# Expert loops: register loads of the experts' numbers without range checks, and from a shifted copy of the table on two engines

## The reference, cut to what matters

```python
# L0: 8 experts, 2 chosen, hidden 256
probs = softmax(tokens @ router_w.T); rw, re = top_k(probs, 2); rw = rw / rw.sum(-1)
out = tokens
for e in range(8):
    out = out + combine[:, e:e+1] * (gelu(tokens @ w1[e] + b1[e]) @ w2[e] + b2[e])

# L1: 32 experts, 1 chosen, hidden 64
idx = argmax(xf @ router_w.T + router_b)
out = relu(relu(xf @ W1[idx] + b1[idx]) @ W2[idx] + b2[idx])

# L3: 16 experts, 2 chosen, hidden 512
topk_vals, topk_idx = top_k(x @ gate_w + gate_b, 2); topk_w = softmax(topk_vals)
y = x + sum_k topk_w[k] * (relu(x @ w1[e_k] + b1[e_k]) @ w2[e_k] + b2[e_k])
out = layernorm(y) * gamma + beta
```

## Time and profile before

| | |
|---|---|
| time of the kernel before, median of 3 runs | 3055.85 us (3051.97 to 3062.43) |
| the profiled execution: its span, first to last instruction | 3096.4 us |
| expert loop of m0, from the first product's start on | about 1199 to 1368 us of the span |
| expert loop of m1, scatters included | about 1847 to 1953 us |
| expert loop of m3 | about 2785 to 3030 us |
| TensorE busy over the whole span | 2449.8 us (79%) |
| GpSimd / VectorE / ScalarE busy | 1747.5 / 1477.2 / 1096.0 us |

### The profile page before, as it was taken

How to read it: one execution, slowest core, us unless ns; L and a number is a source line. 1 busy time by engine, 2 the same in 40 slices (tenths; PEclk the granted TensorE clock), 3 DMA queues, 4 the chain that set the end, 5 groups by cost and what they waited for, 6 DMA issues and landing times. The chain is left out here.

```text
span 3096.4 us, 41425 instructions
## 1 busy us (share of the span) xinstructions
PE 2449.8 (79%) x12303; PEld 1613.2 (52%) x12304; DVE 1477.2 (48%) x4878; ACT 1096.0 (35%) x2433; POOL 1747.5 (56%) x1310
## 2 busy tenths in 40 slices
PE   3344438999999985757979959599897999959994
PEld 1122213444455454656858845387465454548883
DVE  8899976655432255236553452533335000163335
ACT  7799962232210023334433323332334000022223
POOL 4887878888887854657848723485510300034443
PEclk9999999999999997978989969799998999969997
DMA  9989969998869952244535433453402544166664
GB/s 325 298 277 298 277 195 280 278 267 233 202 117 312 291 156 69 85 144 123 112 87 124 91 96 89 143 120 73 124 1 66 163 125 136 52 222 198 200 200 143
DMA packets 391819, 525.78 MB, mean 170 GB/s; under 512 B 161964, under 2 KB 302554, under 8 KB 381645
## 3 DMA queue, kind: packets, MB, share of 16 engines
q1 hardware_dynamic: 238142, 460.63, 43.9%
q0 software_dynamic: 127728, 41.96, 13.6%
q10 hardware_dynamic: 25760, 20.90, 2.0%
HBM read 346.64 MB, written 176.71 MB: 169 GB/s over the span
## 5 line engine op out<-in xcount | busy, mean ns | idle before, releaser
L658 POOL DMA_INDIRECT table_pairs<-sums,index_to x392 | 626.4, 1598 | 164.4 <-issue 120.0
L658 POOL DMA_INDIRECT table_t<-sums,index_from x392 | 619.4, 1580 | 122.7 <-issue 118.6
L1708 PE MATMUL sum_psum<-wide,parts 128*128 128x512 f32 x1800 | 434.0, 396 | 6.9 <-DVE parts L1744 3.0
L1708 PEld LDWEIGHTS sum_psum<-wide,parts 128*128 128x128 f32 x1800 | 342.1, 190 | 81.7 <-DVE parts L1744 3.9
L1264 PE MATMUL sum_psum<-abuf,y 128*128 128x512 f32 (+1 forms) x700 | 305.9, 572 | 28.8 <-DMA abuf<-table_pairs 26.5
L1264 PE MATMUL sum_psum<-abuf,acc 128*128 128x512 f32 (+1 forms) x700 | 296.4, 563 | 0.4 <-ACT partial L1217 0.3
L977 PE MATMUL sum_psum<-abuf,y 128*128 128x512 f32 (+1 forms) x700 | 272.5, 549 | 17.9 <-ACT y L868 17.9
L534 PE MATMUL merge_psum<-part,acc 128*128 128x6 bf16 x980 | 71.0, 167 | 239.3 <-DVE pass_on L608 147.1
L1570 ACT ACTIVATE wide<-abuf 128x512 fp32r<-128x512 f16 (+1 forms) x264 | 148.6, 573 | 250.9 <-PE sum_psum L1708 226.3
L534 PEld LDWEIGHTS merge_psum<-part,acc 128*128 128x128 bf16 x980 | 56.9, 104 | 322.5 <-issue 320.2
L2424 PE MATMUL m_x_yp<-m_kept_w,m_x_h 128*128 x736 | 188.5, 394 | 37.5 <-ACT m_x_h L2485 24.8
(11 more groups left out here) (507 smaller groups left out, 4346.6 us busy)
## 6 DMA issues: line engine op xcount, KB each, us to landing
abuf<-table_pairs SPq DMA_DIRECT2D x240, 512.0 KB
table_pairs<-zero SPq DMA_DIRECT2D x50, 1600.0 KB
abuf<-table_counts SPq DMA_DIRECT2D x90, 640.0 KB
table_t<-zero SPq DMA_DIRECT2D x25, 1600.0 KB
abuf<-table_t SPq DMA_DIRECT2D x150, 256.0 KB, 2.7
m_x_wa<-in_L_ffn_w_dram SPq DMA_DIRECT2D x64, 512.0 KB
table_counts<-peeled ACTq DMA_DIRECT2D x150, 128.0 KB
tokens<-y SPq DMA_DIRECT2D x15, 640.0 KB
```

The costliest lines, as they stand in the source:

```text
L658: nc.gpsimd.indirect_dma_start(table[:, :], bass.IndirectOffsetOnAxis(ap=index[:, g, j:j + 1], axis=0), k.sums[:, g, j, 0:width], None, co ...
L1708: mm = nc.tensor.matmul(k.sum_psum[:, b % 2, f, 0:n], parts[:, v, c, f * P:(f + 1) * P], k.wide[:, j % WIDENED, 0:n], start=(c == 0 and v ...
```

## The change

It does three things.

1. `experts_from` and `values` pass a reason to skip the run-time range checks. The checks behind every register load of m0, m1 and m3 go, on all engines.
2. A second table `k.slot_late` holds the same numbers one element later, written by a second VectorE operation in `route` (m0 and m3). TensorE and VectorE load from it at c, which gives them the numbers of the tiles c - 1 to c + 2. The first load of each loop still comes from `k.slot_expert`. The wait that stood behind the single write of the table goes as well; a later wait covers both.
3. ScalarE in m0 loads eight numbers instead of six (`DEEP + DEEP * held`).

```diff
@@ route @@
-                    link(nc.vector.tensor_scalar(k.slot_expert[0:1, 0:m.tiles], rt_psum[0:1, 0:m.tiles], float(E - 1), None,
-                                                 ALU.min))
+                    for to in (k.slot_expert[0:1, 0:m.tiles], k.slot_late[0:1, 1:1 + m.tiles]):
+                        nc.vector.tensor_scalar(to, rt_psum[0:1, 0:m.tiles], float(E - 1), None, ALU.min)\
+                            .then_inc(s["split"], 1)
+                    link.n += 2
@@ run_experts @@
-    def experts_from(engine, c, most=DEEP):
+    def experts_from(engine, c, most=DEEP, late=False):
 
         count = min(most, n - c) if isinstance(c, int) else most
+        table = k.slot_expert if not late else k.slot_late
         return nc.values_load_multi_w_load_instructions(
-            k.slot_expert[0:1, bass.ds(c, count)], engines=[engine], min_val=0, max_val=E - 1)[1]
+            table[0:1, bass.ds(c, count)], engines=[engine], min_val=0, max_val=E - 1,
+            skip_runtime_bounds_check_because=CLAMPED)[1]
...
-                        experts[:] = [None] * start + list(experts_from(mybir.EngineType.PE, c if start else c - 1))
+                        experts[:] = [None] * start + list(experts_from(mybir.EngineType.PE, c, late=not start))
...
-                        experts[:] = experts_from(mybir.EngineType.Activation, c, DEEP + SOONER * held)
+                        experts[:] = experts_from(mybir.EngineType.Activation, c, DEEP + DEEP * held)
...
-                        experts[:] = [None] * start + list(experts_from(mybir.EngineType.DVE, c if start else c - 1))
+                        experts[:] = [None] * start + list(experts_from(mybir.EngineType.DVE, c, late=not start))
@@ run_pairs @@
         return nc.values_load_multi_w_load_instructions(table[0:1, c:c + min(DEEP, n - c)], engines=[engine], min_val=0,
-                                                        max_val=top)[1]
+                                                        max_val=top, skip_runtime_bounds_check_because=CLAMPED)[1]
@@ build @@
         k.slot_expert = held(ctx, "slot_expert", [1, SLOT_TILES], I32)
+        k.slot_late = held(ctx, "slot_late", [1, SLOT_TILES + 2], I32)
```

More of the change, by code:

```diff
@@ L73 @@
 LN_EPS = 1e-5
+CLAMPED = "the tables hold whole numbers from 0 to the bound for any input"
 def over(eng, n, ways, body, last_apart=False, peeled=1):
```

## The result

The changed kernel takes 3032.2 us (median of 4 runs, 3030.7 to 3040.4), the kernel before 3053.9 us (3051.9 to 3062.4): ratio 0.9934, interval 0.992 to 0.9949, which is some 20 us less (16 to 24). The prediction was 3029 us, and 26.5 us less.

What follows compares the result with a forecast made beforehand. TensorE was taken to bound m3 and mostly m1, engines waiting for each other m0. Gains of 10.8 (m3) + 8 (m1) + 13 (m0) = 31.8 us, less a sixth, 26.5, gave 3029 us from 3055.85; range 3010 to 3046.

Steps and rivals of the forecast that it cites:

- the sixth taken off: Whole sum: part of the gain may exist in the profile alone, so 31.8 us was cut to 26.5 us.
- The further 1 us at the ends: m3: SyncE's first checks (some 0.9 us) and the last single loads' checks (0.5 us) are partly on the path.
- the queue covers 1.6 us: m3: a TensorE block of 2.25 us costs 0.65, the queue hides 1.6; a block of about 0.45 us is covered whole.
- The lower bound of 4 us: m3: least gain, if checks run shorter when nothing is recorded, so most of the block is already covered.
- 4 + 1 + 3 us: m1: 4 from steps with loads before the first scatter, 1 from TensorE's first checks, 3 from waits between scatters.
- GpSimd becomes the bound at 1.27: m1: without stalls TensorE needs about 1.34 us a pair, so GpSimd's 1.27 us soon bounds; 3 of 7.4 us taken.
- m0's term: m0: 12 us, half of the 23 us above GpSimd's floor, plus 1 us at the start: 13 us.
- A: Rival: gain mostly recording, checks cost much less in a plain run; 11 us gained, 3045 us; chance 0.22.
- B: Rival: m0 falls to GpSimd's floor and gives 23 us; sum 42 to 46 us, 3012 us; chance 0.10.
- C: Rival: TensorE's and VectorE's loads stay long despite the shifted table, m0 gets 6; 21 us gained, 3035 us; chance 0.08.
- D: Rival: m0 slower by TensorE's clock, falling to 1.2 GHz as it idles behind GpSimd; 3069 us; chance 0.03.
- one, two and three pieces: Register loads: lengths of 0.3, 0.75 and 1.0 us read as that many pieces, aligned four, aligned six, misaligned four.

Runs made afterwards that it cites:

- experiments 6 to 10: Ratios to the kernel before: only checks removed 0.9937, only table shifted 0.9967, TensorE in m3 alone 0.9961; changed kernel with two TensorE loads in m3 0.9965, first form 0.9926.
- second profile of before: The kernel before, unchanged, timed and profiled again: 3052.3 us, ratio 1.0001, profile span 3051.6 us; the first profile, which the prediction read, had 3096.4 us.

## Why the prediction was right, and where it was not

**The total** was forecast 6.5 us too good, 26.5 us against 20. That it came so near is partly luck. The terms were 10.8 + 8 + 13 = 31.8 us, and measured are about 10, 7 and 1.6. What brought the sum closer was the sixth taken off, for a gain that exists in a profile alone; the runs show no such gain in m3 or m1, but one odd execution.

**m3, right in mechanism and size.** The 15 stalls of 0.65 us are 9.8 us; measured 9.6 to 10.2 us in the loop and 11.6 (7.0 to 16.5) in the timed runs. The further 1 us at the ends isn't there: up to the first product there is no difference, and from the last first product to the end of the last scatter it is 7.1 us in every profile. The step "the queue covers 1.6 us" was the one that carried it, and experiments 6 to 10 measure 1.7. What the text left unsaid follows from it: 0.6 us less of block would have been enough. The lower bound of 4 us, checks that run shorter in a plain run, has no support.

**m1, right in mechanism.** Of 4 + 1 + 3 us the first was 3.6 (first product to first scatter 58.0 us in the second profile of before, 54.4 after), the second 1.1 (the start, above), the last 2.3 (34.12 to 31.86): 7.0 in the profiles, 7.3 (4.3 to 10.4) timed. The step "GpSimd becomes the bound at 1.27" was wrong. The 7.4 us of waits between scatters, of which 3 were taken, were 34.1 - 30.5 = 3.6 us in an undisturbed execution.

**m0, wrong: the failed step.** "The loop takes 169/56 = 3.02 us a tile [...] no more than 23 us are to be had", and half of it taken. The floor was right: 146 us for GpSimd; from the first gather to the last scatter the second profile of before took 148.2 us, the profile after 146.9. The 169 us was not what the kernel does. The loop gave nothing, and only the 1 us said to be won at the start came, as 1.6. The text saw the sign, 40.5 us of span above the median, and spread it evenly ("I take a sixth off"), where 38 of 44.8 us lay in two loops. It should have asked which loop can hold such an excess: hardly m3 with TensorE busy 97%, but m0 with nothing full, and m0's distance from its own floor, 23 us, was of the excess's size. The trace at hand could have said more. The text saw one of GpSimd's waits without a register load near it, and took half; it named the 36.7 us of TensorE's waits as what counts the blocks, where some 21 us of them stood in steps without any load. By this m0's term is near 0, and the other two, 18.8 us with nothing taken off, are the forecast.

**The rivals.** A said 3045 us for another reason, checks that cost less in a plain run; that is not so in m3 and m1, but its guess of m0, 3 us, was nearest. B came true in one sense only: m0 runs at GpSimd's floor, before the change too, so there was nothing to win, although the first two profiles show it as a fall of 28 us. C is refuted by the loads of 0.34 us. The Trainium skill's rule that C drew on (Runtime: NRT & Kernel Launch, Instruction fetch mechanics: some 200 ns per register even in bulk), which that page gives for registers filled from HBM, doesn't carry over to these loads: four numbers took 0.34 us, eight 0.55. D did not come: m0's clock is 0.97, and was 0.96 in the second profile of before.

**What would show it.** The loads, the steps of 3.74 us and the missing checks came as said. The forecast that m0's loop would be "147 to 160 us" and GpSimd's wait for VectorE 10 to 25 us rested on the odd execution; the measured 138.5 and 6.4 us would have been taken for a large success, had the loop of before not been measured again. As forecasts of the changed kernel both were misses.

## What to carry to other kernels

Compare the profiled execution's span with the timed runs first. If it is longer by more than their spread, take the profile again. Until then suspect the loops in which no engine is full (here 38 of the 44.8 us lay in m0 and m1), and count such a term at what the loop's floor and the excess leave. Sort the waits before charging them to a cause: a wait in a step that doesn't hold the suspected instruction isn't its cost. A sequencer's work costs only what goes beyond the queue ahead of it: here the queue covered 1.7 us, so 2.27 us left TensorE idle for 0.58 and 1.60 us cost it nothing, and in m3 removing half was as good as removing all. In m0, where another engine sets the pace, removing all of it gave the loop nothing. An edit meant to add a cost should be looked for in the trace, as an unused load may be gone.

## What the runs showed of the hardware

A register load's time goes by how its numbers lie, not by how many there are. From a multiple of four: four numbers 0.30 to 0.34 us, eight 0.55 us, six 0.76 us. From three past one, four take 1.0 us. Eight took less time than six. An account that fits all four, worked out from these numbers and tried on no other: an aligned group of four is one piece, every other number is a piece of its own, 0.31 us for the first piece and some 0.23 for each further one (six is 4 + 1 + 1, three pieces; the misaligned four is four pieces). By this account the prediction's one, two and three pieces for 0.3, 0.75 and 1.0 us were a wrong reading, and so were its 0.75 us for ScalarE's load of eight.
